# First expert unit placed behind block 15, with that block's transposes, norm and routing inside it, and a reordered opening

## What is computed

```python
mod = (silu(c) @ wmod).reshape(4, 6, 1, 512)          # c (4, 512)
sa, ca, ga, sb, cb, gb = mod[:, 0] ... mod[:, 5]      # ga, gb: sign kept, |.| at least 0.25
h = layernorm(x) * (1 + ca) + sa                      # x (4, 2048, 512) f32
xn = h / |h| * sqrt(512) * gamma
q, kv, a = split(xn @ w_qkva.T)                       # w_qkva (1536, 512)
s[t] = sigmoid(a[t]) * s[t-1] + kv[t]                 # scan over the 2048 tokens
x = x + ga * q * s
h = layernorm(x) * (1 + cb) + sb
p, e = top_k(softmax(h @ Wr), 2)                      # 8 experts, 320 slots per expert and batch
y = relu(h @ W1[e] + b1[e]) @ W2[e] + b2[e]           # W1 (8, 512, 2048), W2 (8, 2048, 512)
out = x + gb * sum over the two chosen of p * y       # tokens beyond the 320 slots are dropped
```

## Time and profile before

| | |
|---|---|
| median of 3 runs | 2404.59 us (2403.39 to 2405.29) |
| profiled execution, its time | 2403.74 us |
| its span | 2401.9 us |
| mean granted TensorE clock | 0.972 |
| PE busy | 2252.1 us, 94% |
| DVE busy | 1228.3 us, 51% |
| ACT busy | 935.6 us, 39% |
| Pool busy | 390.4 us, 16% |

### The profile page before, as it was taken

How to read it: one execution, slowest core, us unless ns; L and a number is a source line. 1 busy time by engine, 2 the same in 40 slices (tenths; PEclk the granted TensorE clock), 3 DMA queues, 4 the chain that set the end, 5 groups by cost and what they waited for, 6 DMA issues and landing times.

```text
span 2401.9 us, 34124 instructions
## 1 busy us (share of the span) xinstructions
PE 2252.1 (94%) x13591; PEld 1263.6 (53%) x13591; DVE 1228.3 (51%) x2209; ACT 935.6 (39%) x1931; POOL 390.4 (16%) x334
## 2 busy tenths in 40 slices
PE   3699999999719999999999999999999999999997
PEld 0244455545316565564656656465565646556563
DVE  4388899989745244343524434352443435335242
ACT  3256657665315052332514234251432425233250
POOL 1013333433230101001010100201110020111102
PEclk8799999999859999999999999999999999999999
DMA  9658899897445323404221340431224043122402
GB/s 250 146 137 200 193 219 222 189 221 192 105 88 175 60 45 75 104 12 110 82 43 45 76 106 10 116 94 25 56 64 106 10 119 94 22 67 53 110 16 33
DMA packets 312551, 245.40 MB, mean 102 GB/s; under 512 B 250983, under 2 KB 250983, under 8 KB 305732
## 3 DMA queue, kind: packets, MB, share of 16 engines
q1 hardware_dynamic: 290488, 200.55, 33.6%
q0 software_dynamic: 21760, 42.14, 9.1%
q10 hardware_dynamic: 144, 0.52, 0.6%
HBM read 105.15 MB, written 93.01 MB: 83 GB/s over the span
## 4 chain that ended last, share of the span: by engine, by line
PE 89%; DVE 3%; DMA 3%; SPq 2%; issue 1%; ACT 1%; POOL 1%; POOLq 0%; ACTq 0%; DVEq 0%
PE bank L1308 35%; PE bank L1294 32%; PE bank L1253 20%; PE bank L1214 1%; SPq L385 1%; DMA reg_e<-reg_a 1%; PE bank L1223 1%; DVE wmx L1075 1%; ACT reg_b L717 1%; DMA reg_e<-slot_rows 1%; DMA reg_e<-reg_e 1%; PE bank L1185 1%; SPq L393 0%; DMA reg_d<-in_wmod 0%; DMA reg_d<-in_w 0%
## 5 line engine op out<-in xcount | busy, mean ns | idle before, releaser
L1294 PE MATMUL bank<-reg_e,reg_a 128*128 128x320 f16 x6144 | 840.8, 299 | 27.2 <-issue 22.6
L1308 PE MATMUL bank<-reg_b,reg_c 128*128 128x512 f16 x3840 | 831.4, 379 | 0.0
L1294 PEld LDWEIGHTS bank<-reg_e,reg_a 128*128 128x128 f16 x6144 | 601.0, 98 | 266.7 <-issue 22.7
L735 ACT ACTIVATE reg_e<-bank,b1s 128x320 f32<-128x320 f32 x512 | 272.0, 531 | 1077.7 <-issue 744.7
L1308 PEld LDWEIGHTS bank<-reg_b,reg_c 128*128 128x128 f16 x3840 | 375.7, 98 | 450.5
L1253 PE MATMUL bank<-reg_c 128*128 128x512 f16 x2304 | 511.8, 381 | 29.1 <-DMA reg_c<-reg_a 29.1
L1153 DVE TENSOR_TENSOR reg_c<-reg_e,reg_c 128x320 f16<-128x320 f32 x512 | 250.4, 491 | 364.2 <-ACT reg_c L736 362.6
L1253 PEld LDWEIGHTS bank<-reg_c 128*128 128x128 f16 x2304 | 224.2, 98 | 292.3 <-issue 37.2
L1129 DVE SCALAR_TENSOR_TENSOR reg_e<-bank,inv,reg_e 128x512 f32<-128x512 f32 x80 | 60.1, 751 | 597.4 <-PE bank L1308 597.4
L568 POOL DMA_INDIRECT out_dram<-reg_e,midx x80 | 166.9, 2086 | 1090.2 <-DVE reg_e L1133 1030.0
L736 ACT ACTIVATE reg_c<-bank,b1s 128x320 f16<-128x320 f32 x512 | 272.7, 533 | 0.0
(11 more groups left out here) (166 smaller groups left out, 1085.9 us busy)
## 6 DMA issues: line engine op xcount, KB each, us to landing
reg_d<-in_w SPq DMA_DIRECT2D x68, 1024.0 KB, 5.6
slot_rows<-reg_d SPq DMA_DIRECT2D x32, 645.0 KB, 8.1
reg_b<-in_x SPq DMA_DIRECT2D x16, 1024.0 KB, 11.7
out_dram<-reg_b SPq DMA_DIRECT2D x16, 1024.0 KB, 11.3
reg_d<-in_wmod SPq DMA_DIRECT2D x4, 1024.0 KB, 22.3
reg_e<-mod_rows SPq DMA_DIRECT2D x7, 512.0 KB, 4.7
reg_e<-in_wq SPq DMA_DIRECT2D x4, 768.0 KB, 12.9
reg_b<-in_wmod SPq DMA_DIRECT2D x2, 1024.0 KB, 30.5
```

Source lines behind the costliest of these rows:

```text
L735: a.activation(rt[:, i % 4, :], src, ACT.Relu, bias=bias, scale=HID_SHIFT).then_inc(s_r, 1)
L1294: ins = mm(bank_h[i % 4][:, 0:CAP], w1s[:, ws, kc, hb * P:(hb + 1) * P], xT[:, u, 4 * xs + kc, b * CAP:(b + 1) * CAP], start=kc == 0 and w ...
L1308: ins = mm(bank_y[i % 2][:, :], hid[:, hs, hc, t * P:(t + 1) * P], w2s[:, ws, hc, :], start=hc == 0 and hs == 0 and ws == 0, stop=hc == HC ...
```

## The change

The diff moves work between stages; the products of attention and experts are the same.

Opening: `mod_spread(0)` and `mod_spread(1)` multiply with a stationary operand that repeats batch 0's column in 128 columns, so the two rows come out on all partitions; ACT and DVE copy them to `mods`. Products 0 and 1 are made again in step 0, for `modr`. DVE does `apply1` of block 0 before it reduces the attention weight, and `lo1(0)` before the low parts. The fills take their data from one row tile `zrow` on 128 partitions and are two transfers each (256 rows and 64 rows); those of batch 0 are issued in step 0, the others four in each of steps 1 to 6. W1 of expert 0 is loaded in step 0, reduced at the ends and middles of steps 0 and 1 with its maximum over partitions taken by a PE transpose (`pm_reduce`, `pm_copy`), its high parts are made in steps 3, 4, 5 and 14.

Join: `attn_steps` runs 16 steps. Scan and sigmoid buffers of the last blocks lie in free x buffers, so unit 0's rows (`xT0`) are loaded at the head of SP's step 15. PE starts unit 0 behind block 15, and `last_block` puts the rest between its half-tiles.

Experts: W2's reduces, scale and split of expert 0 are put later in unit 0 (`W2_MAX`, `W2_SCALE`, `W2_HI`, `W2_LO`), a dummy `partition_all_reduce` stands before, and the loads and splits for a ninth expert are gone.

```diff
-            for i in range(NB + 2):
+            for i in range(NB):
                 step(i // 4, i % 4, i)
...
             def fill(e, b):
-                slots = rows[e * SLOTS + b * CAP:e * SLOTS + (b + 1) * CAP, :]
-                sp.dma_start(slots.rearrange("(p r) n -> p (r n)", p=ZP), ztile[b % 2 * ZP:(b % 2 + 1) * ZP, :].bitcast(I32)).then_inc(s_init, 16)
-
-            sp.wait_ge(s_zrow, 1)
-            for e in range(E):
-                fill(e, 0)
...
+                s0 = e * SLOTS + b * CAP
+                z0 = b % 2 * (P // 2)
+                half, whole = (s0, s0 + P // 2) if z0 else (s0 + 2 * P, s0)
+                sp.dma_start(rows[whole:whole + 2 * P, :].rearrange("(t p) n -> p t n", p=P),
+                             zrow[:, :].unsqueeze(1).to_broadcast([P, 2, ROW // 2])).then_inc(s_init, 16)
+                sp.dma_start(rows[half:half + P // 2, :], zrow[z0:z0 + P // 2, :]).then_inc(s_init, 16)
...
             sp.wait_ge(s_modmm, 5)
             load_x(0, 2)
...
                 if i == 0:
+                    for e in range(E):
+                        fill(e, 0)
                     sp.wait_ge(s_modmm, 6)
                     load_x(0, 3)
+                    for c in (2, 3, 0, 1):
+                        sp.wait_ge(s_modmm, 8 if c < 2 else 6)
+                        sp.dma_start(stage[:, c, :], w1[0, c * P:(c + 1) * P, :]).then_inc(s_stg[c], 16)
+                    sp.dma_start(b1r[:, :], b1[0, :, :]).then_inc(s_b1, 16)
...
+                if i == NB - 1:
+                    sp.wait_ge(s_scn, KC * (NB - 1))
+                    for k in range(2):
+                        sp.wait_ge(s_send[k], 16 * 2 * TB * NB // 4)
+                    load_unit(0, 0)
...
-                if q < B - 1:
-                    fill(2 * j, q + 1)
-                    fill(2 * j + 1, q + 1)
+                if 1 <= i <= 6:
+                    for e in range(4):
+                        fill(4 * ((i - 1) % 2) + e, (i + 1) // 2)
```

SP's order in the expert stage, Pool's at its head:

```diff
+            def experts():
+                load_w2(0)
+                out_rows(NB - 1)
+                turn_h(B - 1, BPB - 1)
+                sp.wait_ge(s_h1, TB * NB)
+                load_b(0)
+                load_gb()
+                for k in range(2):
+                    sp.wait_ge(s_send[k], 16 * 2 * TB * NB // 2)
+                sp.wait_ge(s_xt, 16)
+                load_unit(1, 1)
+                load_w1(1)
...
+            rstd2(NB - 1)
+            g.partition_all_reduce(pmy[:, 1:2], pmy[:, 0:1], P, ABSMAX).then_inc(s_warm, 1)
+            scatter(NB - 2)
+            all_max(0, 1)
+            scatter(NB - 1)
+            for k in range(4):
+                pool.wait_ge(s_out[k], 16 * BPB)
```

DVE and PE:

```diff
+            dve.wait_ge(s_silc, 1)
+            v_.tensor_copy(silcb, silc[:, :, 0:1].to_broadcast([P, KC, P])).then_inc(s_silb, 1)
+            dve.wait_ge(s_modmm, 2)
+            v_.tensor_scalar(mods[:, 1, :], bank[1][:, :], 1.0, None, ALU.add).then_inc(s_modc, 1)
+            dve.wait_ge(s_modc, 1)
+            apply1(0, 0, 0)
+            apply1(0, 0, 1)
...
                 if i == 15:
+                    wait(dve, s_xn, 16 * TB * NB)
                     for c in range(4):
                         w_lo(0, 0, c)
...
+            def last_block(i):
+
+                n, q, j = NB - 1, B - 1, BPB - 1
+                if i == 0:
+                    for t in range(TB):
+                        add_y(n, j, t)
+                if i == 3:
+                    apply2(q, j, 0)
+                if i == 5:
+                    route_choose(q, j - 1)
+                if i == 7:
+                    apply2(q, j, 1)
+                if i == 9:
+                    route_place(q, j - 1)
+                if i == 11:
+                    lo2(n, j)
+                if i == 22:
+                    route_choose(q, j)
+                if i == 28:
+                    route_place(q, j)
...
+            def mod_spread(m):
+
+                wm = stage[:, m, :].rearrange("p (c n) -> p c n", c=KC)
+                pe.wait_ge(s_wmod[m], 16)
+                for c in range(KC):
+                    ins = mm(bank[m][:, :], silcb[:, c, :], wm[:, c, :], start=c == 0, stop=c == KC - 1)
+                ins.then_inc(s_modmm, 1)
...
+                    if i == 0 and k == 4:
+                        mod_mm(0)
+                    if i == 0 and k == 6:
+                        pe.wait_ge(s_modc2, 4)
+                        mod_mm(1)
...
+            def last_block(hb):
+
+                if hb == 0:
+                    for t in range(TB):
+                        turn_y(B, 0, t, NB)
+                if hb == 2:
+                    for t in range(TB):
+                        logits(NB - 2, B - 1, BPB - 2, t)
+                if hb == 5:
+                    positions(NB - 2, B - 1, BPB - 2)
+                if hb == 10:
+                    for t in range(TB):
+                        logits(NB - 1, B - 1, BPB - 1, t)
+                if hb == 13:
+                    positions(NB - 1, B - 1, BPB - 1)
```

More of the change, by code:

```diff
@@ new lines, in load_w2, with load_b @@
+            def load_w2(e):
+                for c in range(4):
+                    wait(sp, s_wlo, 8 * e + c + 1)
+                    sp.dma_start(stage[:, c, :].rearrange("p (c d) -> p c d", c=4),
+                                 w2[e, c * 4 * P:(c + 1) * 4 * P, :]
+                                 .rearrange("(c p) d -> p c d", p=P)).then_inc(s_stg[c], 16)
+            def load_b(e):
+                if e + 1 < E:
+                    wait(sp, s_b1s, e + 1)
+                    sp.dma_start(b1r[:, :], b1[e + 1, :, :]).then_inc(s_b1, 16)
+                wait(sp, s_yd, 2 * UT * e + 2)
+                sp.dma_start(b2t, b2[e:e + 1, :].to_broadcast([P, D])).then_inc(s_b2, 16)
@@ new lines, in load_w1, with next_unit, load_gb @@
+            def load_w1(e):
+                for c in range(4):
+                    wait(sp, s_wlo, 8 * e - 4 + c + 1)
+                    sp.dma_start(stage[:, c, :], w1[e, c * P:(c + 1) * P, :]).then_inc(s_stg[c], 16)
+            def next_unit(v):
+                wait(sp, s_mm1, 2 * HC * (v - 1))
+                wait_alone(sp, s_meta, v - 1)
+                wait_alone(sp, s_xt, 16 * v)
+                load_unit(v, v % 2)
+            def load_gb():
+                sp.wait_ge(s_lg, TB * NB)
+                sp.wait_ge(s_h2, TB * NB)
@@ L559, in _, with scatter @@
             attn_steps(step)
+            def scatter(n):
+                q, j = n // 4, n % 4
+                wait_alone(pool, s_rt, rt_at(q, j) + NRT + (j == BPB - 1))
+                for k in range(2):
+                    for t in range(TB):
+                        g.indirect_dma_start(
+                            out=rows, out_offset=bass.IndirectOffsetOnAxis(ap=sli[:, j % 2, k, t:t + 1], axis=0),
+                            in_=rowi[:, j % 2, t, :], in_offset=None, bounds_check=NSLOTS - 1,
+                            oob_is_err=False).then_inc(s_send[j % 2], 16)
+            rstd2(NB - 1)
[5 more added lines that the diff above has]
+                pool.wait_ge(s_out[k], 16 * BPB)
             for e in range(E):
                 for u in range(2):
-                    all_max(e + u, 1 - u)
+                    if (e or u) and e + u < E:
+                        all_max(e + u, 1 - u)
                     for t in range(UT):
@@ L1107, in w_lo @@
                 if which == 0:
-                    hi, lo = w1s[:, 0, c, :], w1s[:, 1, c, :]
+                    hi, lo = w1s[0][:, c, :], w1s[1][:, c, :]
                 else:
                     hi, lo = (w2s[:, s, 4 * c:4 * c + 4, :].rearrange("p c d -> p (c d)") for s in range(2))
+                if e == 0 and which == 1 and c == 0:
+                    for k in range(4):
+                        dve.wait_ge(s_out[k], 16 * BPB)
                 v_.scalar_tensor_tensor(lo, stage[:, c, :], wsc[:, which:which + 1], hi,
```

384 lines of the change are left out of this document (219 added, 165 removed).

## The result

| | before | after |
|---|---|---|
| median of the runs | 2403.99 us (2401.49 to 2405.29, 4 runs) | 2329.04 us (2327.37 to 2330.57, 4 runs) |
| profiled execution: time, span | 2403.74, 2401.9 | 2330.57, 2328.7 |

The ratio is 0.9689, 95% interval 0.9673 to 0.9706: 3.1% faster. The forecast was 2328, the range 2314 to 2352. The span fell by 73.2 us, against 76.5 in the sum.

What follows compares the result with a forecast made beforehand. PE was taken as full except in the opening and a hole at the join, 600 to 720 us. Terms -25.8 + 12.6 - 15.5 - 52.4 + 4.6 = -76.5 us gave 2328 us, range 2314 to 2352.

Steps and rivals of the forecast that it cites:

- The opening: Before block 0: spread products replace the broadcast transfer, so block 0 starts at 57.6 instead of 83.4, 25.8 us gained.
- Steps 0 to 6: Early attention steps: repeated products 8.5, block 1's transposes 1.5, add_y 1.6 and fills 1, together 12.6 us lost.
- add_y behind the reduces: Early attention steps: DVE's reduces of two W1 quarters stand ahead of block 0's add_y, 1.6 us lost.
- Block 15's step: End of attention: with W1's maximum, scale and high parts made earlier, the step keeps 34.38 us, 15.5 us gained.
- The join: Between block 15 and the first expert unit: gap falls from 62.4 to 10.0 us, 52.4 us gained.
- Unit 0: First expert unit: cold clock 2.0, new PE work 4.8 and stalls 3 make it 113.9 us, 4.6 us lost.
- The upper bound: Stalls in the first expert unit: taken as 3 us, with bounds 0 and 12.
- Units 1 to 15: Remaining expert units: each keeps its 104.1 us, no gain or loss.
- A: Rival, blocks 1 to 7: late DMA queue holds up transposes, 15 to 25 us of gain lost, 2343 to 2353; chance 0.17.
- B: Rival, first expert unit: starves behind DVE or block 15's transposes, 9 to 15 us more, 2337 to 2343; chance 0.10.
- C: Rival, steps 1 to 6: fills move as slowly as the broadcast, some 100 GB/s, kernel slower than before; chance 0.03.
- D: Rival, join: first unit's rows come late, so it doesn't start directly behind; 20 of 52.4 us lost, 2348; chance 0.03.

Runs made afterwards that it cites:

- turn_first: Changed kernel with SP issuing block 0's transposes before it waits for modulation product 4 and loads x block 2: median 2320.75 us, ratio 0.9662.
- max_earlier: Changed kernel with W1 quarters 2 and 3 reduced ahead of step 0's last mix instead of behind it: median 2327.96 us, ratio 0.9695.
- w1_late: Changed kernel with W1 of expert 0 reduced and scaled in step 14 and its high parts made in step 15 again: median 2339.36 us, ratio 0.9739.
- lo_between: Changed kernel with W1's four low parts spread over DVE's step 15 instead of behind the last mix: median 2321.0 us, ratio 0.9663.
- no_dummy: Changed kernel without the dummy all-reduce on Pool: median 2340.65 us, ratio 0.9735.
- fills_64: Changed kernel with every slot fill taken from 64 partitions, same bytes and transfers: median 2354.21 us, ratio 0.9791.
- lo_turn: Changed kernel with two edits, lo_between's and turn_first's: median 2306.82 us, ratio 0.9596.
- best3: Changed kernel with three edits together, those of lo_between, turn_first and max_earlier: median 2300.35 us, ratio 0.9572.

## Why the prediction was right

- **The opening** was right in kind and its gain 2.9 us too high in this execution: block 0 starts at 60.48, not 57.6. In the six other runs with the same opening it starts at 58.1 to 60.4, as the first sixteen spread products take 8.5 to 10.0 us. The spread products ended 1.2 later than products 0 and 1 had, so the reduces ended at 33.82 and not 32.6; products 2 to 4 took 13.0 us, not 12.1; the transposes 8.46, not 7.73. turn_first shows that the wait which I accepted as given, for product 4 before them, cost 12.8 us (60.48 to 47.70).
- **Steps 0 to 6**: 12.6 counted, 13.7 measured, from block 0's start to step 14's logits (510.8 us, before 497.1). That 12.6 was near is in part luck. The first stretch, up to the logits at 158.03, lost 16.3 (97.6 against 81.3), where 11.6 were counted: the repeated products cost the 8.5 as said, block 1's transposes nothing instead of 1.5, and the term that I mis-sized is add_y behind the reduces, 1.6 counted and some 6 measured. The two reduces took 4.5 us, as said, but DVE came to them late: behind its last mix, at 107.24, stand four gate operations and the routing constants, 2.6 us. PE waited 5.19, and the next 8 transposes took 1.94 in place of 1.04, at a granted clock of 0.50. max_earlier takes this away, and the logits come 6 earlier. The steps behind, for which 1 was counted as lost, gained 2.5, and no term of the sum has that: the kernel before had two steps of 36.0 and 36.1, with a wait of 1.42 us for a transfer (the row of the kernel before is below) and slower products behind it, and the changed kernel has 34.8 and 34.7 there. So the fills cost 0.7 at most, with a DMA share of 1.01: step 0's ran at 345 GB/s, a little above what I took (2.0 us each is 330).

```profile
200.62 1.34 PE L1223 MATMUL bank<-wrs,reg_e 128*128 128x8 f16 x48 [1.42 <-DMA reg_e<-reg_e]
```

- **Block 15's step** keeps 34.57 us, 15.3 saved, 15.5 counted. w1_late gives 49.86 back.
- **The join** has one gap, 9.95, ended by DVE's low parts: 10.0 counted. lo_between shows that nothing stands behind it.
- **Unit 0** took 113.05, 113.9 counted. Stalls were 1.8 for ACT and 1.0 for DVE. The upper bound was needed: ten versions of the same unit took 113.8 to 117.8, and no_dummy 124.4, outside the 122.9 that the bound of 12 us of stalls gives; without the pause of 2.8 it would have been inside. My price for a slow all-reduce, DVE 6 us later, was too low, and the room of 13 us that I gave PE against DVE did not cover it: block 15's positions are a product that PE takes in its own order and that needs DVE's routing at once (7.44 us of wait), so DVE's delay of 8.61 came through to PE whole, 8.7.
- **Units 1 to 15**: 1574.8 us before and after, nothing, as said.
- **Rivals.** A fell (period 34.4 to 34.8 in the steps with fills), and fills_64 shows it for the old shape of fills: 2354. B fell here, and no_dummy is near it: 2341. C fell: 345 GB/s against the 100 that it needs. D fell with lo_between. The mechanism was right, but that 2328 and 2329.04 are only 1 us apart is in part luck. The span missed by 3.3: the opening gave 2.9 less and the attention steps took 1.1 more (4.7 in the first stretch, less the 2.5 gained behind it and the 1 counted for the fills), while unit 0 took 0.9 less, without the pause that eleven of thirteen versions have. And I put the median 0.85 us over the profiled execution, where it lay 1.5 under it.

## What to carry to other kernels

When a wait is filled, look at what is queued between the last producer and the consumer in that engine's program: four instructions behind a last mix, two reduces before an add, or a queue's wait for a product that its next transfer doesn't need, cost 10, 6 and 13 us here, and moving each was an edit of a few lines. Judge such an edit by the start of the next stage in the trace as well as by the median: 15 us won at the start of unit 0 showed as 8. And run the small edits together before giving one up; max_earlier alone was not worth its measurement, and with lo_between it takes 4.5 us more off (2321.0 to 2316.5), with lo_turn 6.5 (2306.8 to 2300.35).

## What the hardware showed that was not expected

- Writes of zero rows from 64 partitions ran at 209 GB/s, the same bytes from 128 partitions at 345, over the same stretch of 66 to 82 us. That the rows of the tile are read several times over showed no cost: the old fills, which read each row once, had 212.
- Full DMA engines (share 1.01 over 34.5 us) did not lengthen a step; at the rate of the narrow fills the same bytes did, by 22.5 us over six steps.
- A first all-reduce on Pool held DVE for 6.58 us in the kernel before and 8.61 in no_dummy; a dummy ahead of the row writes took it off DVE's path, and the row writes did not bring it back (0.7 at most).
- ACT leaves finished half-tiles lying for 3.0 to 5.0 us (its idle time of 4.44 to 6.52 less the usual 1.48), and PE stops for 0.6 to 2.2, without a cause in the trace, always near block 15's logits in unit 0: in all versions run but the changed kernel and best3.
